# Single PSUM banks for score pairs, one exponential of 512 columns for each row half, and a rearranged table of steps

## The chip, the cores and the metric

The kernel runs on one core of a Trainium2 chip. The metric is the device time of one execution in microseconds (us). Shown are the median of timed runs and one profiled execution, whose trace the rows below are read from.

## What is computed

Four attention blocks one after the other on eight images of 32x32 tokens with 128 channels, all in float32. The first two blocks have 8 heads of 16 channels behind a group norm, the last two have one head over all 128 channels, behind a layer norm and a group norm:

```python
x = _L0_conv_ref(...)   # group norm, 8 heads: softmax(q k / 4) v, projection, + x
x = _L1_conv_ref(...)   # group norm, 8 heads, biases, + the normed x
x = _L2_conv_ref(...)   # layer norm, 1 head of 128 channels, + x
x = _L3_conv_ref(...)   # group norm, 1 head of 128 channels, + x

scores = jnp.einsum('bcq,bck->bqk', q, k) * hd ** (-0.5)
scores = jax.nn.softmax(scores, axis=-1)
o = jnp.einsum('bqk,bck->bqc', scores, v)
```

## The kernel before

A class `Plan` writes down one order of work for the whole kernel, and every engine's program walks that same list, taking from it what is its own; semaphores tie them together. The table `STEPS` is that order, one letter a step: T a score tile, P a pair, V the values of a slot, U half of them (half the columns), and C the next of everything else that the plan lists. `arranged` deals the items out by these letters.

The blocks with heads are 16 stages (an image in a block) of 4 rounds. A round is 4 heads of one half of the queries; it has 32 tiles and 8 slots. A **tile** (L1376) is one matmul on one half of the array's rows, giving scores of 128 queries by 512 keys; VectorE takes its row maxima (L1168). When a round's tiles are done, the negated maxima are turned (`shift`), split in two by ScalarE and VectorE, and written by SyncE's queue into rows of `q_stack` (four transfers, L853), where the next matmuls add them to the scores. A slot is one block of 128 keys: two **pairs**, each two matmuls (L1404), one on either half of the rows, for two heads by 512 queries. ScalarE takes the exponential of a pair, 1024 columns in one instruction (L1057), and the **values** (L1430) multiply the four probability blocks of a slot into `outs`, on four column strips side by side. The order of a pair's halves is chosen (`rows_first`) so that halves alternate along TensorE's stream and two neighbouring matmuls run side by side.

The blocks with one head are image-wide stages: **scores** (L1448, six matmuls of two halves), a maximum over 1024 columns (L1200), an exponential with its sum (L1064), eight transposes as a **turn** (L1292), a copy by ScalarE (L1073), the **pv** steps (L1470) and an output `y` by VectorE. They lie between the stages with heads, and the last 200 us hold nothing else. **Chunks** (L1292 to L1355) are the norms and projections of all blocks; their results are taken by ScalarE or VectorE.

The kernel uses eight PSUM banks of 512 columns. Three are `work`, handed out in turn to tiles, shifts, small chunks and some projections (`in_work`). Four are `pairs`, two buffers of two banks, handed out in turn to pairs, scores, turns and the other chunks (`in_pairs`); a projection of 512 columns takes a whole buffer and uses its first bank. One is `outs`. `count` gives each item its buffer and remembers who had it before; `wait_for_bank` and `wait_for_pairs` make TensorE wait until that one's reader has finished. So pair t waits for one exponential, that of the pair before it in its buffer.

## Time and profile before

| | us |
|---|---|
| median of 3 runs | 2158.66 |
| lowest, highest | 2158.46, 2170.19 |
| the profiled execution | 2159.86 |
| its span, first to last instruction | 2158.1 |

The profile gives, for this one execution, the busy time of every engine (PE is TensorE, PEld its weight loads, DVE VectorE, ACT ScalarE, POOL GpSimd, SP SyncE), who ended each wait, and the chain of work that ended last. TensorE's matmuls overlap and their ends are modelled: what a step costs is read from the start of one to the start of the next. A gap of a weight load is not time lost by itself, since loads run beside matmuls. The table of stretches has the granted clock of TensorE in its last columns but two, as a share of full speed.

### The profile page before, as it was taken

To read this page: it belongs to the slowest core of one execution; us is meant where nothing else is said; L and a number is where in the kernel's file an instruction comes from. 1 tells how busy PE (TensorE), PEld (TensorE's weight loads), DVE (VectorE), ACT (ScalarE), POOL (GpSimd) and SP (SyncE) were. 2 spreads that over 40 slices of the span, in tenths; PEclk is the share of its full clock that TensorE was granted. 3 is DMA by queue.
4 is the path that set the end of the run, shared out by engine and by line. 5 is a ranking of instruction groups with operands and counts; after the bars stand their busy time and mean duration, and the time that the engine had idled before them with its cause. 6 is when DMAs were issued, how large, how long until landed. Compare 5 with 4: busy or idle time off the path is not lost.

```text
span 2158.1 us, 39609 instructions
## 1 busy us (share of the span) xinstructions
PE 2096.4 (97%) x15750; PEld 1168.3 (54%) x15750; DVE 1687.8 (78%) x3104; ACT 1447.0 (67%) x1698; POOL 408.0 (19%) x541
## 2 busy tenths in 40 slices
PE   4999999999999999999999999999999989999999
PEld 2444444444744467444764448644584336746888
DVE  6899999999799867887679886898778957763433
ACT  1477777777577755887458874688647865586554
POOL 3102111220122311122120221213111040130221
PEclk7799999999999999999999999999999999999999
DMA  5322241331222314041230503204040050000000
GB/s 144 70 31 66 48 96 46 65 72 29 55 55 56 45 31 79 12 85 16 55 65 2 99 2 70 50 2 99 1 103 7 2 99 1 11 2 1 11 1 20
DMA packets 48583, 97.34 MB, mean 45 GB/s; under 512 B 7824, under 2 KB 10640, under 8 KB 48272
## 3 DMA queue, kind: packets, MB, share of 16 engines
q1 hardware_dynamic: 48400, 94.81, 21.0%
q8 instruction: 126, 2.06, 0.4%
q14 instruction: 57, 0.47, 0.1%
HBM read 55.98 MB, written 37.75 MB: 43 GB/s over the span
## 4 chain that ended last, share of the span: by engine, by line
PE 84%; DVE 8%; DMA 2%; issue 2%; ACT 2%; POOL 1%; SPq 1%; POOLq 0%; DVEq 0%; ACTq 0%
PE outs L1430 21%; PE work L1376 17%; PE pairs L1404 12%; PE outs L1470 11%; PE pairs L1448 8%; DVE part_max L1168 6%; PE pairs L1292 6%; PE pairs L1298 3%; PE pairs L1301 2%; PE work L1298 2%; DMA q_stack<-shift_parts 2%; PE work L1301 2%; ACT probs L1057 1%; DVE neg_max L1200 1%; SPq L853 1%
## 5 line engine op out<-in xcount | busy, mean ns | idle before, releaser
L1168 DVE TENSOR_REDUCE part_max<-work 128x1 f32<-128x512 f32 x2048 | 1282.7, 681 | 176.1 <-PE work L1376 169.6
L1057 ACT ACTIVATE probs<-pairs 128x1024 f32<-128x1024 f32 x1024 | 1002.1, 1023 | 261.2 <-PE pairs L1404 244.4
L1376 PE MATMUL work<-k_stack,q_stack 62*128 62x512 f32 x2048 | 609.7, 453 | 5.9 <-DVE part_max L1168 3.8
L1430 PE MATMUL outs<-probs,v_heads 128*32 128x512 f32 (+1 forms) x5216 | 565.8, 512 | 0.8 <-DVE o_turn L1180 0.2
L1404 PE MATMUL pairs<-q_stack,k_stack 64*128 64x512 f32 x2048 | 509.0, 446 | 15.4 <-DMA q_stack<-shift_parts 14.0
L1376 PEld LDWEIGHTS work<-k_stack,q_stack 62*128 62x128 f32 x2048 | 286.9, 187 | 316.3 <-DVE part_max L1168 233.0
L1404 PEld LDWEIGHTS pairs<-q_stack,k_stack 64*128 64x128 f32 x2048 | 224.9, 185 | 220.1 <-ACT probs L1057 128.8
L1200 DVE TENSOR_REDUCE neg_max<-pairs 128x1 f32<-128x1024 f32 x128 | 156.7, 1224 | 207.4 <-PE pairs L1448 206.7
L1064 ACT ACTIVATE probs<-pairs,neg_max 128x1024 f32<-128x1024 f32 x128 | 142.8, 1116 | 241.0 <-DVE neg_max L1200 241.0
L1470 PEld LDWEIGHTS outs<-v_full,probs 128*128 128x128 f32 x2048 | 250.8, 191 | 37.3 <-issue 28.8
L1470 PE MATMUL outs<-v_full,probs 128*128 128x128 f32 x2048 | 269.7, 279 | 0.2
L1430 PEld LDWEIGHTS outs<-probs,v_heads 128*32 128x32 f32 x5216 | 114.1, 108 | 195.2 <-issue 174.0
L1448 PE MATMUL pairs<-k_full,q_full 128*128 128x512 f32 x768 | 211.6, 411 | 4.3 <-ACT probs L1064 1.9
L945 POOL TENSOR_TENSOR o_both<-o_turn,o_inv 128x256 f32<-128x256 f32 x64 | 39.8, 621 | 752.8 <-DVE o_inv L1183 752.8
L1073 ACT COPY probs<-pairs 128x1024 f32<-128x1024 f32 x128 | 129.8, 1014 | 49.9 <-PE pairs L1292 49.8
L1448 PEld LDWEIGHTS pairs<-k_full,q_full 128*128 128x128 f32 x768 | 134.7, 188 | 49.5 <-issue 12.9
L1292 PE MATMUL pairs<-avg,probs 128*128 128x128 f32 x1024 | 133.5, 273 | 0.1
L1292 PEld LDWEIGHTS pairs<-avg,probs 128*128 128x128 f32 x1024 | 116.3, 141 | 17.6 <-issue 16.5
L967 POOL CAST parts<-parts 128x512 fp32r<-128x512 f32 x64 | 39.3, 614 | 265.9 <-ACT parts L1028 265.9
L903 POOL TENSOR_TENSOR rstd<-var_eps,minus_half 128x1 f32<-128x1 f32 (+1 forms) x32 | 26.7, 835 | 298.2 <-DVE var_eps L1131 242.6
L969 POOL TENSOR_TENSOR parts<-parts 128x512 fp32r<-128x512 f32 x64 | 82.0, 1280 | 5.1
L1180 DVE STREAM_TRANSPOSE o_turn<-outs 128x512 f32<-128x512 f32 x64 | 45.3, 708 | 9.5 <-PE outs L1430 9.5
(128 smaller groups left out, 1157.2 us busy)
## 6 DMA issues: line engine op xcount, KB each, us to landing
k_scratch<-parts SPq DMA_DIRECT2D x64, 256.0 KB
q_scratch<-parts SPq DMA_DIRECT2D x64, 256.0 KB
k_stack<-k_scratch SPq DMA_DIRECT2D x64, 256.0 KB, 6.9
q_stack<-q_scratch SPq DMA_DIRECT2D x64, 256.0 KB, 9.6
k_stack<-k_scratch SPq DMA_DIRECT2D x64, 128.0 KB, 8.1
q_stack<-q_scratch SPq DMA_DIRECT2D x64, 128.0 KB, 10.2
q_stack<-shift_parts SPq DMA_DIRECT2D x256, 4.0 KB
tmp<-x SPq DMA_DIRECT2D x7, 512.0 KB, 3.8
```

Of the source, the lines that this page charges most:

```text
L1057: nc.scalar.activation(probs[:, plan.prob[u], 2 * n:2 * n + 2, :], pairs[:, plan.half["pair", t], :, :], ACT.Exp, scale=HEAD_SCALE).then_i ...
L1064: nc.scalar.activation(p_full[:, n % 2, :], bank_of(("scores", n)), ACT.Exp, bias=neg_max1[:, n % SUMS:n % SUMS + 1], accum_out=sum1[:, n ...
L1073: nc.scalar.copy(pT_full[m % 2][:, :, P * (n % 2):P * (n % 2 + 1)], bank_of(("turn", n)).rearrange("p (k q) -> p k q", q=P)).then_inc(f_co ...
L1168: nc.vector.tensor_reduce(part_max[:, r % 2, column:column + 1], bank_of(("tile", r, n)), AX_X, ALU.max, negate=True).then_inc(tile_max, 1)
L1200: nc.vector.tensor_reduce(neg_max1[:, n % SUMS:n % SUMS + 1], bank_of(("scores", n)), AX_X, ALU.max, negate=True).then_inc(f_max, 1)
L1292: last = nc.tensor.transpose(bank[:, P * n:P * (n + 1)], source(j), ident)
L1298: return nc.tensor.matmul(to, weights, moving, start=True, stop=True)
L1376: nc.tensor.matmul(bank_of(("tile", r, n)), qs[rows, i, a, heads, P * t:P * (t + 1)], ks[rows, i, keys, heads, :], start=True, stop=True). ...
L1404: last = nc.tensor.matmul(pairs[:, plan.half["pair", t], half, :], ks[rows, i, key // QT, first + n, P * (key % QT):P * (key % QT + 1)], q ...
L1430: last = nc.tensor.matmul(outs[2 * HD * n:2 * HD * (n + 1), columns], v_heads[:, i, key, at:at + 2 * HD], probs[:, plan.prob[u], n, column ...
L1448: last = nc.tensor.matmul(pairs[:, plan.half["scores", n], half, :], q_full[:, k % 2, q, queries], k_full[:, k % 2, key, columns_of(half)] ...
L1470: last = nc.tensor.matmul(outs[:, P * j:P * (j + 1)], pT_full[m % 2][:, k, P * j:P * (j + 1)], v_full[:, at % 2, k, :], start=k == 0, stop ...
```

## The change

The seven banks that are not `outs` become one tensor `banks`. A class `Banks` hands them out, the longest unused first, by kind of item and by part of the order. In the stages with heads ("head"), tiles and their like take one of banks 4 to 6, and each half of a pair takes one of banks 0 to 3 by itself, as does a projection of 512 columns; wide chunks take two neighbours. In the image-wide stages ("full"), scores, turns and wide chunks take banks 0 and 1 or 2 and 3, a pair there takes such a double, one bank for each half, and projections go with the tiles.

A pair's halves each wait for their own bank and each count in `pair_full`; ScalarE takes one exponential of 512 columns for each half, in the order in which the matmuls come, and each counts in `exp_done`. What waits for these two semaphores waits for doubled counts.

The table of steps is rearranged, and scores (S), turns (R), pv steps (G) and y (Y) have letters of their own. Both tables hold the same items; the values split in two number 140 before and 128 after. The table is cut here to a few of its lines.

```diff
-WORK_BANKS = 3
+BANKS = 7
+SINGLES = {"head": {"work": (4, 5, 6), "exp": (0, 1, 2, 3)}, "full": {"work": (4, 5, 6)}}
+DOUBLES = {"head": ((0, 1), (1, 2)), "full": ((0, 1), (2, 3))}
...
+class Banks:
+
+    def __init__(self):
+        self.holders, self.last, self.count = [None] * BANKS, [-1] * BANKS, 0
+
+    def take(self, choices, holder):
+
+        chosen = min(choices, key=lambda banks: max(self.last[b] for b in banks))
+        before = []
+        for b in chosen:
+            if self.holders[b] is not None and self.holders[b] not in before:
+                before.append(self.holders[b])
+            self.holders[b], self.last[b] = holder, self.count
+        self.count += 1
+        return chosen, before
+
+    def take_for(self, plan, item, part):
+
+        if item[0] in ("scores", "turn"):
+            return [self.take(DOUBLES["full"], item)]
+        if item[0] == "pair" and part == "full":
+            (first, second), before = self.take(DOUBLES["full"], (*item, 1))
+            self.holders[first] = (*item, 0)
+            return [((first,), before), ((second,), before)]
+        if item[0] == "pair":
+            return [self.take([(b,) for b in SINGLES[part]["exp"]], (*item, k)) for k in range(2)]
+        if plan.in_pairs(item) and item[1] not in HALVES:
+            return [self.take(DOUBLES[part], item)]
+        user = "exp" if plan.in_pairs(item) and part == "head" else "work"
+        return [self.take([(b,) for b in SINGLES[part][user]], item)]
+
+
+def part_of(item, part):
+    return "full" if item[0] in ("scores", "turn", "pv") else "head" if item[0] == "values" else part
...
     STEPS = (
-        "TPTTPV TPTTPTV TPTPUTTU TPTPUTTU CTPTPTV TPTTUPTTU TTPPTTV CPPTTTUU PTTUTPTU TTPPTUTTU PPTTTV TTPPTV "
...
+        "TPTTPV TPTTPTV TPTPUTTU TPTPUTTU CTPTPTV TPPTTTUTTU TPPTTUU CTPPTTV PTTUTPTU TPPTTUTPTU TTPPTV TTPTV "
...
+        "PTTPV PTTTPV CSV CSTR CTTTR CTTSGSGTTTGR GSGGSGGR YTTGCGTTGGR GSGTTTGGCCYSGTTTGR GCGCR SGTTGCGTTGCR "
+        "YSGTTTGGCCGCR SGGGTTTGCYR SGGGTTGCCTTCCGR SGGTTTGCCR YSTTTGCSGR TTTGGGGGGR YTTGSTTGCCGGR TTPGGGGTYTR "
...
+        "GGCSGGGYSGCGSGGCR GGGGCYR CSGSGGGR CGCGCGCCGR YR GGGSCSGGGGR GYSGGSGGR GGGGR YCSGGGGR CSGGGGR YCCSGGGGR "
+        "CSGGGGR YCCCCSGGGGR CCSGGGGR YSGGGGR SGGGGR YSGGGGR SGGGGR YSGGGGR SGGGGR YSGGGGR GGGGR YGGGGGGGGY "
     )
...
-        queues = {n: deque(c for c in order if n == self.class_of(c)) for n in "TPC"}
+        queues = {n: deque(c for c in order if n == self.class_of(c)) for n in "TPCSRGY"}
...
-        return {"tile": "T", "pair": "P", "values": "V"}.get(item[0], "C")
+        return {"tile": "T", "pair": "P", "values": "V", "scores": "S", "turn": "R", "pv": "G", "y": "Y"}.get(item[0], "C")
...
-            if self.in_work(item):
-                bank = n % WORK_BANKS
-                n += 1
-                self.bank[item], self.before[item] = bank, held.get(bank)
-                held[bank] = item
-            elif self.in_pairs(item):
-                self.half[item] = ring % 2
-                ring += 1
-                self.pairs_before[item] = pairs_held.get(self.half[item])
-                pairs_held[self.half[item]] = item
+            part = part_of(item, part)
+            if self.in_work(item) or self.in_pairs(item):
+                taken = banks.take_for(self, item, part)
+                self.banks[item] = sum((chosen for chosen, _ in taken), ())
+                self.before[item] = [before for _, before in taken]
...
-        pairs = psum("pairs", [P, 2, 2, HALF])
+        banks = psum("banks", [P, BANKS, HALF])
         outs = psum("outs", [P, HALF])
-        work = psum("work", [P, WORK_BANKS, HALF])
...
-            if item in plan.bank:
-                return work[:, plan.bank[item], :]
-            both = pairs[:, plan.half[item], :, :]
-            return both[:, 0, :] if item[0] == "chunk" and item[1][-1] in "01" else both.rearrange("p a k -> p (a k)")
+            first, last = plan.banks[item][0], plan.banks[item][-1]
+            if first == last:
+                return banks[:, first, :]
+            return banks[:, first:last + 1, :].rearrange("p a k -> p (a k)")
+
+        def halves_of(t):
+
+            first = plan.rows_first["pair", t]
+            return first, 1 - first
...
-                        sp.wait_ge(pair_full, 2 * STAGE_SLOTS * (g - 1))
+                        sp.wait_ge(pair_full, 4 * STAGE_SLOTS * (g - 1))
...
-                    act.wait_ge(pair_full, t + 1)
-                    nc.scalar.activation(probs[:, plan.prob[u], 2 * n:2 * n + 2, :],
-                                         pairs[:, plan.half["pair", t], :, :], ACT.Exp,
-                                         scale=HEAD_SCALE).then_inc(exp_done, 1)
+                    for k, half in enumerate(halves_of(t)):
+                        act.wait_ge(pair_full, 2 * t + k + 1)
+                        nc.scalar.activation(probs[:, plan.prob[u], 2 * n + half, :],
+                                             banks[:, plan.banks["pair", t][k], :], ACT.Exp,
+                                             scale=HEAD_SCALE).then_inc(exp_done, 1)
...
+                def wait_for_banks(item, k=0):
+                    for before in plan.before[item][k]:
+                        if before[0] == "tile":
+                            pe.wait_ge(tile_max, plan.tile_nth[before] + 1)
+                        elif before[0] == "pair":
+                            pe.wait_ge(exp_done, 2 * before[1] + before[2] + 1)
+                        elif before[0] == "scores":
+                            pe.wait_ge(f_exp, before[1] + 1)
+                        elif before[0] == "turn":
+                            pe.wait_ge(f_copied, before[1] + 1)
+                        elif before[0] == "shift":
+                            pe.wait_ge(*taken(*before))
+                        else:
+                            pe.wait_ge(*taken(*before[1:]))
...
-                    wait_for_pairs(("pair", t))
-
-                    start = plan.rows_first["pair", t]
-                    for half in (start, 1 - start):
+                    for k, half in enumerate(halves_of(t)):
                         rows = slice(ROWS * half, ROWS * (half + 1))
-                        last = nc.tensor.matmul(pairs[:, plan.half["pair", t], half, :],
-                                                ks[rows, i, key // QT, first + n, P * (key % QT):P * (key % QT + 1)],
-                                                qs[rows, i, a, first + n, :], start=True, stop=True)
-                    last.then_inc(pair_full, 1)
+                        wait_for_banks(("pair", t), k)
+                        nc.tensor.matmul(banks[:, plan.banks["pair", t][k], :],
+                                         ks[rows, i, key // QT, first + n, P * (key % QT):P * (key % QT + 1)],
+                                         qs[rows, i, a, first + n, :], start=True, stop=True).then_inc(pair_full, 1)
...
-                    pe.wait_ge(exp_done, 2 * (u + 1))
+                    pe.wait_ge(exp_done, 4 * (u + 1))
```

## Rows read from the trace of the kernel before

**Rows 1.** The page: the span and the busy time of each engine.

```profile
span 2158.1 us, 39609 instructions
...
PE 2096.4 (97%) x15750; PEld 1168.3 (54%) x15750; DVE 1687.8 (78%) x3104; ACT 1447.0 (67%) x1698; POOL 408.0 (19%) x541
```

**Rows 2.** The page: the chain that ended last, by engine, then by line.

```profile
PE 84%; DVE 8%; DMA 2%; issue 2%; ACT 2%; POOL 1%; SPq 1%; POOLq 0%; DVEq 0%; ACTq 0%
...
PE outs L1430 21%; PE work L1376 17%; PE pairs L1404 12%; PE outs L1470 11%; PE pairs L1448 8%; DVE part_max L1168 6%; PE pairs L1292 6%; PE pairs L1298 3%; PE pairs L1301 2%; PE work L1298 2%; DMA q_stack<-shift_parts 2%; PE work L1301 2%; ACT probs L1057 1%; DVE neg_max L1200 1%; SPq L853 1%
```

**Rows 3.** Busy time by stretch: stretch, length, us busy of each engine, clock, DMA.

```profile
75.00:500.00 425.00, 419.23 (x3381) 182.96 (x3380) 399.92 (x719) 313.31 (x346) 74.48 (x107) 1.00 0.33 66
...
1400.00:1500.00 100.00, 99.89 (x778) 42.74 (x771) 91.66 (x163) 85.40 (x94) 19.34 (x34) 1.00 0.26 54
```

**Rows 4.** The same for the exponentials of L1057 alone.

```profile
1400.00:1500.00 100.00, 78.93 (x82) 1.00 0.26 54
```

**Rows 5.** Groups by line and shape: count, busy us, mean ns, idle before.

```profile
L1057 ACT ACTIVATE probs<-pairs 128x1024 f32<-128x1024 f32 x1024 | 1002.1, 1023 | 261.2 <-PE pairs L1404 244.4 <-PE outs L1470 11.1 <-PE outs L1430 1.5
...
L1022 ACT COPY v_full<-pairs 128x512 f32<-128x512 f32 x13 | 7.6, 587 | 2.6 <-PE pairs L1301 1.5 <-PE pairs L1298 0.8
...
L1168 DVE TENSOR_REDUCE part_max<-work 128x1 f32<-128x512 f32 x2048 | 1282.7, 681 | 176.1 <-PE work L1376 169.6
```

**Rows 6.** Who waited for whom: us in total, times, longest.

```profile
PEld work L1376 <- DVE part_max L1168: 233.0, 443, 1.2
...
PEld pairs L1404 <- ACT probs L1057: 128.8, 244, 0.9
...
PE pairs L1404 <- DMA q_stack<-shift_parts: 14.0, 6, 8.6
```

**Rows 7.** Timeline near 382 us: start, us, instruction, idle before and releaser.

```profile
380.37 3.77 ACT L1057 ACTIVATE probs<-pairs 128x1024 f32<-128x1024 f32 x4
...
382.36 0.50 PE L1404 MATMUL pairs<-q_stack,k_stack 64*128 64x512 f32 x2 [0.33 <-ACT probs L1057]
```

**Rows 8.** Timeline of TensorE and its weight loads near 408 us.

```profile
401.97 0.64 PE L1430 MATMUL outs<-probs,v_heads 128*32 128x256 f32 x8
...
402.54 0.55 PE L1376 MATMUL work<-k_stack,q_stack 62*128 62x512 f32 x2
...
404.32 0.50 PE L1376 MATMUL work<-k_stack,q_stack 62*128 62x512 f32 x2
...
404.66 0.39 PE L1404 MATMUL pairs<-q_stack,k_stack 64*128 64x512 f32 x2
...
405.21 0.16 PEld L1430 LDWEIGHTS outs<-probs,v_heads 128*32 128x32 f32 x8 [0.36 <-issue]
...
406.21 0.50 PE L1404 MATMUL pairs<-q_stack,k_stack 64*128 64x512 f32 x2
...
406.54 0.39 PE L1376 MATMUL work<-k_stack,q_stack 62*128 62x512 f32 x2
...
412.92 1.07 PE L1430 MATMUL outs<-probs,v_heads 128*32 128x512 f32 x8
...
413.91 0.73 PE L1376 MATMUL work<-k_stack,q_stack 62*128 62x512 f32 x3
```

**Rows 9.** Timeline of TensorE in two image-wide stages.

```profile
1316.71 1.04 PE L1292 MATMUL pairs<-avg,probs 128*128 128x128 f32 x8
...
1317.51 1.63 PE L1448 MATMUL pairs<-k_full,q_full 128*128 128x512 f32 x6
...
2130.95 1.04 PE L1292 MATMUL pairs<-avg,probs 128*128 128x128 f32 x8
...
2131.88 1.66 PE L1448 MATMUL pairs<-k_full,q_full 128*128 128x512 f32 x6
```

**Rows 10.** A long piece of the chain, and timeline at a first pair.

```profile
1227.44 10.40 DMA q_stack<-shift_parts
...
1774.95 0.79 PE L1404 MATMUL pairs<-q_stack,k_stack 64*128 64x512 f32 x2 [8.60 <-DMA q_stack<-shift_parts]
```

148 lines of the change are left out of this document (58 added, 90 removed).

## Prediction

> **What bounds the kernel now.** I read the page first. TensorE is busy 97% of the span, VectorE 78%, ScalarE 67% [rows 1], so TensorE is the bound and every microsecond in which it waits counts in full. Busy TensorE is not TensorE without waits, though: matmuls overlap, and a short wait disappears inside the modelled busy time. The chain that ended last shows what the waits are made of: 84% TensorE, 8% VectorE, 2% DMA, 2% ScalarE; by line the maxima of score tiles (L1168) hold 6% and the exponentials (L1057) 1% [rows 2]. The reader should see that the engine whose instructions are split here, ScalarE, has 1% of the path (some 22 us, between 11 and 32 with the rounding), and that the larger part of the waiting is for VectorE, whose work the change leaves as it is.
>
> The table by stretch says where. From 75 to 500 us VectorE is busy 399.92 of 425 us and TensorE 419.23: two engines nearly full. From 1400 to 1500 it is ScalarE that is fullest, 85.40 of 100 us [rows 3], with 82 exponentials [rows 4].
>
> **ScalarE: one exponential of 1024 columns becomes two of 512.** One of 1024 takes 1023 ns, and a 512-column copy out of the same banks 587 ns [rows 5]. Four exponentials in a row took 3.77 us [rows 7]: taking off one full length for the last, (3.77 - 1.02) / 3 = 0.92 us each, so a follower overlaps by about 0.10. A 512-column exponential should then take 0.59 alone and 0.49 in a row. A pair costs 2 x 0.49 - 0.92 = 0.06 us more where ScalarE is saturated, and at worst, with no overlap, 2 x 0.587 - 1.023 = 0.15. Over 1024 pairs that is 61 to 154 us of ScalarE time, of which I take 61, because the row of four is the case that matters. ScalarE goes from 1447 to about 1510 us, 70% of the span. In the fullest stretch it goes from 85.4 to 85.4 + 82 x 0.06 = 90.3 us of 100. What hides this is ScalarE's own idle time; the cover is gone where the extra reaches (100 - 85.4) / 82 = 0.18 us per pair, beyond the worst case above. So I put nothing on the path for it directly, only through the queue in the next term.
>
> **TensorE: two waits and two increments a pair instead of one.** A score tile already has a wait and an increment for each matmul. Two tiles that open a run took 404.66 - 404.32 = 0.34 us until the next, and the two matmuls of a pair 406.54 - 406.21 = 0.33 [rows 8]. Where both matmuls of a slot wait and count, the slot is no more than 0.01 us longer, so the second wait and increment cost 0 to 10 us over 1024 pairs; I take 0. The Trainium skill speaks against this edit: "TensorE: Matmul & The Clock Gate", section "The cost: per-tile semaphore tail", has increments of matmuls that run side by side serialise at about 26 ns each. An estimate from that page is 1024 x 0.026 = 27 us more; the rows here show at most 0.01 a pair.
>
> **The ring of single banks.** Before, a pair waits until the whole exponential of the pair two before it has ended. At 382.36 a pair waits for L1057 while four exponentials run back to back [rows 7]. After, four banks go round, and the first half's bank comes free about 0.46 us sooner than the second's; the second comes 0.06 later than now. TensorE runs its stream in order, so the wait itself still ends at the second half. What is won is that one of two matmuls is done inside it: at most about half of a 0.33 us step, less the 0.06. With 244 such waits [rows 6], 0.12 - 0.06 gives 15 us if each of them were a real one. They are not: a weight load also stands idle 0.36 us with nothing late [rows 8], and 128.8 - 244 x 0.36 = 41 us is a ceiling that the chain's 22 us lies under. The queue in front of ScalarE grows with its load, against the gain. I take -6 us; the ends are -22 (the whole share of L1057) and +22 (that share doubled). A second gain is structural: a 512-column chunk took one of two double buffers, so that by the old table 114 of 1024 pairs follow the pair directly before them in their buffer and 115 follow a chunk. In the new table, handed out by the new rule, 1573 of 2048 halves follow the fourth half before and 249 the third. Few of those places can cost anything now, since the old order kept them apart; the gain can come only through the order, which is the next term.
>
> **The table.** Tiles keep their pace: counted at every 16th slot of values, both tables have issued the same number of tiles to within 4. So nothing is shifted between stages. Three things change. Values split in two fall from 140 to 128: a half until the next run takes 402.54 - 401.97 = 0.57 us, a whole 413.91 - 412.92 = 0.99 [rows 8], so a split costs 0.15 and twelve give -2 us (0 to -4, if a run of row matmuls is cut besides). Unbroken runs of three tiles fall from 184 to 163; runs of two or more pairs rise from 161 to 185. Three tile banks and 681 ns a maximum make a run of three the place where TensorE waits for L1168. That wait is at most 233.0 - 443 x 0.36 = 74 us [rows 6, 8]; 21 of 184 runs fewer is 11% of it, -8 us. Its ends are 0 and -25, because VectorE has only 25 us of idle time in the first 425 us, where the waits are densest [rows 3]. Third, in the image-wide stages scores, turns, values and outputs now have letters of their own. Before, 105 of 128 score steps take the banks of the score step directly before them and so wait for a maximum and an exponential; after, 60 do, and 50 take a turn's. In the last stretch a turn is followed by scores after 2131.88 - 2130.95 = 0.93 us, where nothing is late after 1317.51 - 1316.71 = 0.80 [rows 9]: 0.13 us a step. 45 steps fewer would be -6; in the middle stages tiles fill part of the wait already, so I take -4 (0 to -11).
>
> **What gets later.** Round 42's shift rows are requested T13 P8 V4 ahead of their first pair where they were T17 P10 V5 ahead: by the steps above, about 0.9 us of row matmuls and 0.99 of values less. Its transfer was 10.40 us on the chain [rows 10] and hardly waited for, so this is +1 to +2, I take +1. Round 59's wait of 8.60 us [rows 10] keeps its distance of P4 V2 in both tables and stays; all such waits together are 14.0 us [rows 6]. The only other edit on SyncE is a count doubled for the doubled increments, at no cost: it is met by the same instruction.
>
> **The sum.** -6 - 2 - 8 - 4 + 1 = -19 us. The profiled execution took 2159.86 us, its span 2158.1; the median of the three runs is 2158.66, 1.2 under it. 2159.86 - 19 - 1.2 gives about 2140. As every term but one is a share of a wait that I could only bound from above, I forecast 2142.
>
> **The rivals.** *A larger gain.* The freer ring lets the new order remove half of what is left of both waits: half of 22 us of exponentials and half of 74 of maxima, 48 us, with the rest as above 2107 to 2125; say 2115. For it speaks that TensorE is the bound, so nothing else takes over; against it that VectorE has 25 us to give in the densest stretch. *Nothing measurable.* The waits that count are VectorE's, with the same three banks and the same 2048 maxima, and ScalarE's share of the path is 1%: the split values and the last stage remain, 2152. *Slower: ScalarE's queue.* Place: the dense head stretches like 1400 to 1500. There ScalarE goes to 90 of 100 us, in the worst case to 85.4 + 82 x 0.15 = 97.7; with runs of pairs up from 161 to 185 each run meets a fuller queue. If the path's share of L1057 doubles and the order brings nothing, 2158.66 + 22 = 2181. It decides from about 0.12 us extra a pair on (95 of 100 us), twice the price that I take. *Slower: the second increment.* If each pair's two increments cost the path what a slot can hide at most, 0.01 us by the rows, it is +10 on the forecast, 2152. An estimate from the Trainium skill's "TensorE: Matmul & The Clock Gate", same section, would make it 2142 + 27 = 2169.
>
> **Chances.** The forecast, a gain of 6 to 21 us, 0.40. The larger gain 0.30. Nothing measurable 0.14. ScalarE's queue 0.12, half of it past 1%. The second increment 0.04. About 1% is what a measurement of this kernel can tell from no change: 21.6 us. Faster by over 1% is all of the larger gain and a small part of the forecast's own spread, 0.34; slower by over 1% is half of ScalarE's queue and a little for what I do not see, 0.10; the rest, 0.56, within 1%. The range has to reach into the larger gain and a little past no change: 2112 to 2168. The forecast's own range is 2137 to 2153.
>
> **What the profile would show.** Right on ScalarE: 2048 exponentials of 128x512 with a mean near 590 ns, ScalarE near 1510 us busy; past 1580, the overlap is gone and the queue rival is alive. Right on the ring: the weight loads of the pairs wait for the exponentials less than 128.8 us in all, and its share of the chain stays at or under 1%. Right on the table: tile weight loads wait for L1168 less than 233.0 us, and in the last 180 us turns are followed by scores after 0.80 rather than 0.93 us. The DMA wait of 8.60 us is still there. I would be wrong if VectorE's share of the chain grows, if the pairs' runs make TensorE wait twice where it waited once (once for each half, with no row matmul of the other half to run beside), or if a transfer of shift rows that landed in time now lands late in more than one round.

## The result: 0.6% faster, and the profile after

The changed kernel takes 2147.98 us (median of 9 runs, 2142.41 to 2153.83) against 2158.66 us (9 runs): a ratio of 0.9942, 95% interval 0.9923 to 0.9961. That lies inside the forecast's own range of 2137 to 2153 us, 6 us above the forecast. The profiled execution took 2149.76 us.

The page of the changed kernel: busy time, then the chain that ended last by engine and by line. L1412 is the score tiles' matmul, L1425 the pairs', L1450 the values', L1092 the exponentials, L1203 the maxima of tiles.

```profile
span 2148.0 us, 40503 instructions
...
PE 2090.5 (97%) x15668; PEld 1166.9 (54%) x15668; DVE 1689.0 (79%) x3104; ACT 1499.1 (70%) x2722; POOL 408.0 (19%) x541
...
PE 86%; DVE 7%; DMA 2%; issue 2%; ACT 1%; SPq 1%; POOL 0%; POOLq 0%; DVEq 0%; ACTq 0%
```

Against [rows 1, 2] ScalarE is 52 us busier, VectorE's and ScalarE's shares of the path are each a point smaller. The groups of the two instructions in dispute, and the table by stretch:

```profile
L1203 DVE TENSOR_REDUCE part_max<-banks 128x1 f32<-128x512 f32 x2048 | 1282.3, 681 | 184.1 <-PE banks L1412 178.3
L1092 ACT ACTIVATE probs<-banks 128x512 f32<-128x512 f32 x2048 | 1063.7, 604 | 198.8 <-PE banks L1425 173.9
```

```profile
75.00:500.00 425.00, 421.45 (x3424) 183.04 (x3420) 402.21 (x725) 331.82 (x639) 75.07 (x108) 1.00 0.33 66
1400.00:1500.00 100.00, 98.60 (x762) 41.66 (x750) 89.58 (x160) 87.78 (x172) 21.65 (x38) 1.00 0.29 54
```

An exponential of 512 columns has a mean of 604 ns, and the group of 2048 is busy 1063.7 us where the 1024 were 1002.1 [rows 5]: 0.06 us more a pair. The dense stretch goes from 85.40 us [rows 3] to 87.78. The waits, us in total, times, longest:

```profile
PEld banks L1412 <- DVE part_max L1203: 248.7, 464, 1.2
PEld banks L1425 <- ACT probs L1092: 139.4, 257, 1.7
PEld outs L1450 <- ACT probs L1092: 48.0, 158, 0.7
...
PE banks L1425 <- DMA q_stack<-shift_parts: 16.3, 6, 8.0
```

Each of these is larger than in [rows 6], and the kernel is faster all the same. The values' wait for exponentials (48.0) was small before:

```profile
PEld outs L1430 <- ACT probs L1057: 13.0, 43, 0.4
```

A weight load that waits while the matmul ahead of it still runs costs nothing, so the sums of this view do not add up to time. For what follows the times come from two other readings. One lays two traces side by side at the same slot of work (the first values of a stage, the same score step) and reads how far apart they are. The other takes the matmuls that start 0.02 to 0.09 us after the instruction that frees their bank, and adds up how far each gap between its start and that of the matmul before goes past 0.12 us, the run of tiles that opens the kernel left out; "bound" below means this count.

**Where the time went.** Side by side, the changed kernel is 5.6 us ahead at the first values of stage 8 (931 us), in the head stages, and 6.7 at those of stage 10. It loses 3.6 us at the first values of round 42 and 1.6 at those of round 50, whose shift rows come late, and is 2.2 us ahead at the last values of the head stages. The last image-wide stages, from score step 88 to 127, take 179.1 us in place of 187.0: that brings it to 10.1.

### The profile page after: what moved, and what is told of

It is laid out like the page before. It is cut to its first block, busy times and chain, and to the rows that moved or that the text cites. A ratio compares the mean times of both kernels' runs of the same rounds, so it can differ in the third digit from the quotient of the medians.

```text
span 2148.0 us, 40503 instructions
## 1 busy us (share of the span) xinstructions
PE 2090.5 (97%) x15668; PEld 1166.9 (54%) x15668; DVE 1689.0 (79%) x3104; ACT 1499.1 (70%) x2722; POOL 408.0 (19%) x541
## 4 chain that ended last, share of the span: by engine, by line
PE 86%; DVE 7%; DMA 2%; issue 2%; ACT 1%; SPq 1%; POOL 0%; POOLq 0%; DVEq 0%; ACTq 0%
PE outs L1450 21%; PE banks L1412 17%; PE banks L1425 12%; PE outs L1490 11%; PE banks L1468 9%; PE banks L1331 6%; PE banks L1337 6%; DVE part_max L1203 5%; PE banks L1340 4%; DMA q_stack<-shift_parts 2%; ACT probs L1092 1%; SPq L887 1%; DVE stats L1141 0%; PE banks L1398 0%; DVE o_turn L1215 0%
## 5 line engine op out<-in xcount | busy, mean ns | idle before, releaser
L1203 DVE TENSOR_REDUCE part_max<-banks 128x1 f32<-128x512 f32 x2048 | 1282.3, 681 | 184.1 <-PE banks L1412 178.3
L1092 ACT ACTIVATE probs<-banks 128x512 f32<-128x512 f32 x2048 | 1063.7, 604 | 198.8 <-PE banks L1425 173.9
L1412 PE MATMUL banks<-k_stack,q_stack 62*128 62x512 f32 x2048 | 638.8, 458 | 4.2 <-DVE part_max L1203 2.0
L1450 PE MATMUL outs<-probs,v_heads 128*32 128x512 f32 (+1 forms) x5120 | 566.0, 520 | 0.6 <-DVE o_turn L1215 0.2
L1425 PE MATMUL banks<-q_stack,k_stack 64*128 64x512 f32 x2048 | 532.9, 440 | 16.9 <-DMA q_stack<-shift_parts 16.3
L1412 PEld LDWEIGHTS banks<-k_stack,q_stack 62*128 62x128 f32 x2048 | 289.4, 187 | 335.3 <-DVE part_max L1203 248.7
L1425 PEld LDWEIGHTS banks<-q_stack,k_stack 64*128 64x128 f32 x2048 | 262.6, 186 | 200.3 <-ACT probs L1092 139.4
L1099 ACT ACTIVATE probs<-banks,neg_max 128x1024 f32<-128x1024 f32 x128 | 142.8, 1116 | 257.7 <-DVE neg_max L1235 213.2
L1235 DVE TENSOR_REDUCE neg_max<-banks 128x1 f32<-128x1024 f32 x128 | 156.7, 1224 | 164.9 <-PE banks L1468 164.3
L1450 PEld LDWEIGHTS outs<-probs,v_heads 128*32 128x32 f32 x5120 | 111.9, 108 | 197.3 <-issue 142.9
L1468 PE MATMUL banks<-k_full,q_full 128*128 128x512 f32 x768 | 209.5, 408 | 1.3 <-ACT probs L1092 0.3
L1468 PEld LDWEIGHTS banks<-k_full,q_full 128*128 128x128 f32 x768 | 134.9, 189 | 36.7 <-issue 9.9
```

The source lines that it names most:

```text
L1092: nc.scalar.activation(probs[:, plan.prob[u], 2 * n + half, :], banks[:, plan.banks["pair", t][k], :], ACT.Exp, scale=HEAD_SCALE).then_inc ...
L1099: nc.scalar.activation(p_full[:, n % 2, :], bank_of(("scores", n)), ACT.Exp, bias=neg_max1[:, n % SUMS:n % SUMS + 1], accum_out=sum1[:, n ...
L1203: nc.vector.tensor_reduce(part_max[:, r % 2, column:column + 1], bank_of(("tile", r, n)), AX_X, ALU.max, negate=True).then_inc(tile_max, 1)
L1235: nc.vector.tensor_reduce(neg_max1[:, n % SUMS:n % SUMS + 1], bank_of(("scores", n)), AX_X, ALU.max, negate=True).then_inc(f_max, 1)
L1412: nc.tensor.matmul(bank_of(("tile", r, n)), qs[rows, i, a, heads, P * t:P * (t + 1)], ks[rows, i, keys, heads, :], start=True, stop=True). ...
L1425: nc.tensor.matmul(banks[:, plan.banks["pair", t][k], :], ks[rows, i, key // QT, first + n, P * (key % QT):P * (key % QT + 1)], qs[rows, i ...
```

## Experiments

The kernel before was run beside each group of kernels; its medians there were 2159.79, 2161.27, 2160.5 and 2159.6 us.

| kernel | us, median (range) | ratio to before, 95% interval |
| --- | --- | --- |
| changed | 2147.98 (2142.41 to 2153.83) | 0.9942 (0.9923 to 0.9961) |
| 1 banks and split, old table | 2166.65 (2163.91 to 2173.75) | 1.0036 (1.0023 to 1.0049) |
| 2 table alone | 2163.36 (2156.37 to 2168.14) | 1.0011 (0.9997 to 1.0024) |
| 3 before, new order at the end | 2152.94 (2146.82 to 2162.97) | 0.9972 (0.9958 to 0.9985) |
| 4 changed, old order at the end | 2149.94 (2147.19 to 2161.56) | 0.9956 (0.9943 to 0.9969) |
| 5 split on doubles | 2171.95 (2168.81 to 2175.54) | 1.0054 (1.0035 to 1.0073) |
| 6 exponentials in quarters | 2174.96 (2173.65 to 2176.35) | 1.0066 (1.0049 to 1.0083) |
| 7 four banks for tiles | 2384.68 (2382.78 to 2386.05) | 1.1035 (1.1014 to 1.1056) |
| 8 shift rows by ScalarE's queue | 2163.45 (2159.56 to 2167.94) | 1.0010 (0.9996 to 1.0025) |
| 9 reads behind the shift rows | 2129.42 (2128.62 to 2130.81) | 0.9848 (0.9827 to 0.9870) |
| 10 unsplit on single banks | 2158.59 (2153.25 to 2165.06) | 0.9986 (0.9972 to 0.9999) |
| 11 before, with the reads of 9 | 2144.82 (2143.53 to 2148.92) | 0.9927 (0.9907 to 0.9947) |
| 12 split on doubles, one wait | 2160.00 (2154.26 to 2163.78) | 0.9998 (0.9982 to 1.0014) |

**1 and 2: the two halves of the change.** Run 1 is the changed kernel with the old table and its letters, run 2 the kernel before with the new ones. The diff is that of run 1, without the table itself; run 2 has the reverse.

```diff
-        queues = {n: deque(c for c in order if n == self.class_of(c)) for n in "TPCSRGY"}
+        queues = {n: deque(c for c in order if n == self.class_of(c)) for n in "TPC"}
...
-        return {"tile": "T", "pair": "P", "values": "V", "scores": "S", "turn": "R", "pv": "G", "y": "Y"}.get(item[0], "C")
+        return {"tile": "T", "pair": "P", "values": "V"}.get(item[0], "C")
```

> The new banks and the two exponentials of 512 columns, with the table of steps of before. Theory: the banks by themselves bring little, because the old order already keeps pairs away from the places where two double buffers run short: 2153 to 2160 us, with the pairs' weight loads waiting 110 to 135 us for the exponentials (128.8 before, 139.4 after) and ScalarE near 1500 us busy. Rival, ScalarE's queue: the dearer exponentials cost the path by themselves, 2163 to 2180 us, and the values' weight loads wait 40 us or more for the exponentials (13.0 before, 48.0 after). Rival, the banks are the whole gain: 2146 to 2150 us.

> The new table of steps and its letters, on the two double buffers and the exponentials of 1024 columns of before. Theory: the order of the image-wide stages gives its gain on any banks (some 8 us in the last of them), but the new order sets pairs where the double buffers run short, and the heads lose what the last stage wins: 2152 to 2165 us, pairs' weight loads waiting for exponentials 150 us or more (128.8 before). Rival, the table is the whole gain and needs no new banks: 2146 to 2151 us. Rival, the table can't do without the banks: over 2170 us.

Neither half is worth anything alone: 7 us slower, and 4 us slower with an interval that holds no change; together 11 us faster. The change is not a sum of its parts.

Side by side, one part does add up: the last image-wide stages take 187.0 us before and in run 1, 179.1 in run 2 and in the changed kernel, so the new order there is worth 7.9 us on any banks. What does not add up is the head stages. At their last values, in one execution of each, run 1 is 10.5 us behind the kernel before, run 2 is 7.3 behind, and the changed kernel is 2.2 ahead. TensorE's waits for shift rows are not the reason: they are longest in the changed kernel (16.3 us, against 14.0 before, 14.8 in run 1 and 10.8 in run 2).

Run 1 lies in the range of the rival of ScalarE's queue, and its sign came too: the values' weight loads wait 46.8 us. But the changed kernel has 48.0 of them and is 18.7 us faster, and counted as bound waits the values come to under 2 us in run 1. So the sign does not show the rival, and no run rules out that ScalarE has a share in the 7 us. The bound waits of TensorE show a part of what happens (count, us in all):

| kernel | pair halves, for exponentials | tiles, for maxima |
| --- | --- | --- |
| before | 105, 15.3 | 137, 27.2 |
| 2 table alone | 137, 30.4 | 114, 22.8 |
| 1 banks alone | 71, 11.1 | 147, 30.8 |
| changed | 80, 12.4 | 130, 25.1 |

On doubles the new table's longer runs of pairs double the waits for exponentials; on single banks it hardly matters how the pairs lie. And the old table loses on single banks in another place. A transposing chunk there takes two neighbouring banks and waits for the later of two pair halves. The waits of that chunk in run 1, then in the changed kernel:

```profile
PEld banks L1332 <- ACT probs L1093: 10.2, 13, 1.5
...
PE banks L1332 <- ACT probs L1093: 4.8, 7, 1.1
```

```profile
PEld banks L1331 <- ACT probs L1092: 5.2, 11, 0.9
```

In run 1 TensorE itself stands still for 4.8 us, in the changed kernel for 0.4. Side by side, run 1 falls behind the kernel before in stages 8, 12, 14 and 15 (1.9, 2.8, 1.6, 2.1 us), and one such wait of a weight load, 0.7 to 1.5 us long, lies in each of them. That is not the whole of it: the kernel before has waits of 0.3 to 0.8 us at the same places, in stage 14 one as long as in run 1, and run 1 also waits longer for shift rows, by 1.1 us in stage 8, 0.9 in stage 12 and 0.4 in stage 14. The rest of its 7 us I cannot place.

**3 and 4: the order at the end.** Run 3 is the kernel before with the new table's order for all that is left after the last values; run 4 is the changed kernel with the old order there. Both deal out both tables and take the second for what the first has not yet issued:

```diff
+    SEGMENTS = [('own', ('values', 511, 0, 2)), ('other', None)]
```

> The kernel before, with its own order up to the last values (slot 511) and from there on the new table's order of what is left; banks and exponentials as before. Theory: the last image-wide stages, from the first to the last scores step after the heads 187.0 us before and 179.1 after in the traces, gain their 8 us from the order alone: 2149 to 2153 us, with scores S88 to S127 in 178.5 to 180 us. Rival, it needs the new banks too, since the projections there go with the tiles' banks: 2155 to 2159 us.

> The changed kernel with its order up to the last values (slot 511) and from there on the old table's order of what is left. Theory: it gives back 7 to 8 us, 2154 to 2157 us, so that banks, exponentials and the order of everything before the last stages are worth 2 to 4 us together. Rival, the last stages gain by the banks: under 2151 us.

The new order at the end is worth 6.9 us on the old banks (2159.79 - 2152.94). Putting the old one back costs 2.0 us where 7 to 8 were expected, and that time lies in the rival's range. The traces decide against the rival: run 3 takes 179.1 us for the last stages and run 4 takes 187.0, so the order is worth 7.9 us there on either banks. Run 4 had made up for it in the head stages, at whose last values it is 9.9 us ahead of the kernel before and the changed kernel 2.2; they have the same order, but run 4 waited 4.5 us less for shift rows (11.8 against 16.3), and what such a wait costs besides is told at run 9. The timeline shows the step that the prediction counted, 0.79 us from a turn to scores instead of 0.93 [rows 9]:

```profile
2024.82 1.04 PE L1331 MATMUL banks<-avg,probs 128*128 128x128 f32 x8
2025.61 1.63 PE L1468 MATMUL banks<-k_full,q_full 128*128 128x512 f32 x6
```

and one that it did not count. TensorE in the kernel before, while a norm is worked out:

```profile
2053.64 0.28 PE L1298 MATMUL work<-mv,avg 128*128 128x1 f32 x2
2055.07 0.35 PE L1298 MATMUL work<-var_in,avg 128*128 128x1 f32 x2 [1.15 <-POOL var_in L915]
2055.28 1.63 PE L1448 MATMUL pairs<-k_full,q_full 128*128 128x512 f32 x6
```

and the same two steps of the norm in the changed kernel, with a turn and values between them:

```profile
2042.36 0.28 PE L1337 MATMUL banks<-mv,avg 128*128 128x1 f32 x2
2042.50 1.07 PE L1331 MATMUL banks<-avg,probs 128*128 128x128 f32 x8
2043.41 1.95 PE L1490 MATMUL outs<-v_full,probs 128*128 128x128 f32 x16
2045.20 0.28 PE L1337 MATMUL banks<-var_in,avg 128*128 128x1 f32 x2
```

With scores, turns, values and outputs as letters of their own, the table can put work into the 1.4 us that the norm takes. The old letter took them all from one queue in the planner's order.

**5, 12 and 10: splitting, and single banks.** All three have the new table. Run 5 gives each pair of the head stages one double of two banks again, with split exponentials:

```diff
-        if item[0] == "pair" and part == "full":
+        if item[0] == "pair":
             (first, second), before = self.take(DOUBLES["full"], (*item, 1))
...
-        if item[0] == "pair":
-            return [self.take([(b,) for b in SINGLES[part]["exp"]], (*item, k)) for k in range(2)]
```

> The changed kernel with one edit: in the head stages a pair takes a double of two banks again, (0,1) or (2,3), and waits for both before its first matmul; the two exponentials, the two increments and the new table stay. Theory A, the single banks are what the new table needs (a half can start while the other half's bank is still held, and a chunk of 512 columns takes one bank and not two): it falls back to about the run of the table alone, 2160 to 2168 us, 10 us or more above the changed kernel, and most of the difference lies before 941 us, where table alone and changed kernel differ by 12.9 us. Theory B, what helps is the split exponential (ScalarE starts half a pair earlier and a half is done sooner): it stays within 3 us of the changed kernel, 2146 to 2151 us. Between the two, 2153 to 2158 us, each has a share.

It came out slower than the table alone and than either theory, and its trace had a flaw of its own: 1862 wait instructions more than needed. Run 12 takes them out:

```diff
                 def wait_for_banks(item, k=0):
+                    if k and plan.before[item][k] is plan.before[item][0]:
+                        return
                     for before in plan.before[item][k]:
+                        if before[0] == "pair" and before[2] == 0 and (*before[:2], 1) in plan.before[item][k]:
+                            continue
```

> The run with split exponentials on doubles again, with its waits put together: there a pair waited for both halves of the pair before, ahead of each of its matmuls, four waits in all (1913 instructions more than the changed kernel), and at 102 pairs the first matmul started 0.12 to 0.15 us after the exponential's end where it is 0.03 to 0.06 in the other kernels. Here one wait, for the later of the two exponentials, stands ahead of the first matmul. Theory A, the doubles themselves cost (release of a whole pair, a chunk of 512 columns taking two banks): the time stays above 2160 us. Theory B, a good part of the 22 us between that run and the changed kernel was the price of the extra waits: it falls to 2150 to 2160 us, and the single banks are worth what is left.

So the waits alone cost 12 us (2171.95 - 2160.00, 6 ns for each on average), and run 5 must not be read as the price of doubles. Splitting alone on doubles is 2163.36 to 2160.00, -3 us with ranges that overlap. Run 10 has single banks and no split where it can be avoided:

```diff
+                    if plan.whole[t]:
+                        act.wait_ge(pair_full, 2 * (t + 1))
+                        nc.scalar.activation(probs[:, plan.prob[u], 2 * n:2 * n + 2, :],
+                                             banks[:, low:high + 1, :], ACT.Exp,
+                                             scale=HEAD_SCALE).then_inc(exp_done, 1)
+                        return
                     for k, half in enumerate(halves_of(t)):
```

> The changed kernel with the exponentials unsplit where they can be: a pair still takes two single banks, one by one, and each half waits for its own bank only, but where the two banks lie side by side (777 of 1024 pairs) one exponential of 1024 columns reads both and gives both back at once; 247 pairs keep two of 512. Theory A, the gain of the single banks is the earlier release of the first half: with it gone for three pairs in four, the kernel loses most of the 22 us by which it beats split exponentials on doubles, and stands at 2156 to 2168 us. Theory B, the gain is that a 512-column chunk takes one bank of four and no double, and the split is only a price (0.25 us for each us of ScalarE by the run with quarters): ScalarE falls from 1499 to about 1460 us and the kernel is 7 to 12 us faster, 2136 to 2141.

Its ScalarE is 43 us less busy than in the changed kernel, and it is 10.6 us slower. By the bound waits of pair halves: table alone 30.4 us, split on doubles 31.7 (158 of them), single banks mostly unsplit 25.0 (123), both 12.4. The reading that fits is that a half that waits for its own bank gains only if that bank's exponential ends earlier, and an exponential that ends earlier only if the bank is handed on by itself. With the new table each of the two is worth 3 to 5 us alone, with ranges that overlap, and together 15.4 (2163.36 - 2147.98). The waits for shift rows speak against this order of the four (10.8, 8.2, 14.5 and 16.3 us) and so do not make it.

**6: ScalarE's price.** Each 512-column exponential is cut into two of 256, and only the second counts:

```diff
-                        nc.scalar.activation(probs[:, plan.prob[u], 2 * n + half, :],
-                                             banks[:, plan.banks["pair", t][k], :], ACT.Exp,
-                                             scale=HEAD_SCALE).then_inc(exp_done, 1)
+                        for c in (slice(0, HALF // 2), slice(HALF // 2, HALF)):
+                            last = nc.scalar.activation(probs[:, plan.prob[u], 2 * n + half, c],
+                                                        banks[:, plan.banks["pair", t][k], c], ACT.Exp,
+                                                        scale=HEAD_SCALE)
+                        last.then_inc(exp_done, 1)
```

> The changed kernel with each 512-column exponential cut once more, into two of 256 columns; only the second one counts, so banks, waits and order are those of the changed kernel and only ScalarE's time goes up. From 1023 ns for 1024 columns and 604 for 512, 256 columns should take 0.39 us, so 0.15 more a half, less what overlaps: ScalarE goes from 1499 to between 1650 and 1800 us. Theory A, ScalarE still has cover: the time rises by at most 5 us, to 2153. Theory B, ScalarE's queue is already on the path in the densest stretches, as the run of the banks alone suggests (52 us more of ScalarE, about 8 us slower, so 0.15 us per us): 150 to 300 us more of ScalarE give 22 to 45 us, 2170 to 2193, and the share of the exponentials in the chain goes past 3%.

ScalarE went to 1606.7 us only, 107.6 more, since followers overlap more than I worked out; the time rose by 27 us, 0.25 us for each us of ScalarE. The chain by engine, and the group:

```profile
PE 80%; ACT 12%; DVE 5%; issue 2%; DMA 1%; POOL 0%; SPq 0%; POOLq 0%; ACTq 0%; DVEq 0%
```

```profile
L1093 ACT ACTIVATE probs<-banks 128x256 f32<-128x256 f32 x4096 | 1178.9, 432 | 135.2 <-PE banks L1427 115.3 <-PE outs L1492 11.6 <-PE outs L1452 0.5
```

ScalarE's share of the path goes from 1% to 12%, and the bound waits of pair halves from 12.4 to 46.7 us. ScalarE's queue was a real danger, 0.105 us a pair (107.6 / 1024) past where the change stopped.

**7: one bank from the pairs to the tiles.**

```diff
-SINGLES = {"head": {"work": (4, 5, 6), "exp": (0, 1, 2, 3)}, "full": {"work": (4, 5, 6)}}
+SINGLES = {"head": {"work": (3, 4, 5, 6), "exp": (0, 1, 2)}, "full": {"work": (4, 5, 6)}}
```

> The changed kernel with one bank moved in the head stages from the pairs to the score tiles: tiles go round over four banks, pair halves over three; the table and the image-wide stages stay. Theory A, a run of three tiles waits because there are three banks (the ground on which the table was to give 8 us): the weight loads of tiles wait for the maxima less than 200 us in place of 248.7, and the kernel is 5 to 20 us faster, 2128 to 2143. Theory B, VectorE's pace and not the depth of its ring sets those waits, and the pairs need their fourth bank: the waits of the tiles fall, those of the pairs for exponentials rise from 139.4 past 200 us, and the kernel is 10 to 40 us slower, 2158 to 2190.

```profile
PEld banks L1425 <- ACT probs L1092: 415.5, 549, 1.2
...
PEld banks L1412 <- DVE part_max L1203: 199.0, 329, 1.0
```

The tiles' waits fall by 50 us, their bound waits from 25.1 to 4.1; the pairs' bound waits rise from 12.4 to 268, and the kernel is 237 us slower, where theory B had said 10 to 40. With three banks a half waits for the exponential of the pair directly before it (397 of the 420 bound waits). Three single banks are too few; with four, two pairs are in flight and 12.4 us of bound waits are left.

**8, 9 and 11: the shift rows.** Run 8 sends the shift rows of ten rounds from ScalarE's queue, two pairs later:

```diff
                         shift(item[1])
+                        if item[1] in OTHER_QUEUE:
+                            due[item[1]] = 2
                     elif kind == "pair":
                         exp(item[1])
+                        for r in list(due):
+                            due[r] -= 1
+                            if due[r] == 0:
+                                send_shift(r, act)
+                                del due[r]
```

> The changed kernel with the shift rows of ten rounds (6, 14, 15, 16, 18, 26, 34, 42, 50, 59: those that follow a large read, load or write closely) sent from ScalarE's queue, two pairs after ScalarE has copied them, in place of SyncE's, where they stand behind that read. Theory A, the waits of first pairs for shift rows (16.3 us in the changed kernel, 8.3 of them in round 59, 3.1 in round 42) lie on the path and come from the place in SyncE's queue: they fall under 4 us and the kernel is 8 to 14 us faster, 2134 to 2140. Theory B, the transfer is late because the DMA engines are busy with the read, whichever queue asks: the waits stay within 4 us of 16.3 and the time within 3 us of 2148.

The kernel is 15 us slower than the changed one, which neither theory had. The waits of rounds 34, 42 and 50 went. But round 59 still waited, and so did round 14 (2.1 us) and round 6, whose rows had gone ahead of the next stage's reads in SyncE's order and were now asked for two pairs later. TensorE's timeline at the first pairs of rounds 6 and 59:

```profile
226.51 0.80 PE L1434 MATMUL banks<-q_stack,k_stack 64*128 64x512 f32 x2 [12.78 <-DMA q_stack<-shift_parts]
...
1785.25 0.80 PE L1434 MATMUL banks<-q_stack,k_stack 64*128 64x512 f32 x2 [6.24 <-DMA q_stack<-shift_parts]
```

ScalarE may pay for sending, too: its next exponential came after 2.43 us of standing idle. For most of that it had no work, since the next pair's matmul started at 213.00 us and took 0.50; some 0.7 us are left for the sending. Its timeline and its queue's (ACTq) at round 6:

```profile
210.90 1.22 ACTq L842 DMA_DIRECT2D q_stack<-shift_parts  x1
...
212.16 1.94 ACTq L842 DMA_DIRECT2D q_stack<-shift_parts  x3
214.21 2.06 ACT L1093 ACTIVATE probs<-banks 128x512 f32<-128x512 f32 x4 [2.43 <-PE banks L1434]
```

So another queue is not enough: the transfers in flight are still there. The busy share of the DMA engines from 190 to 235 us of this run, in tenths, 40 slices:

```profile
DMA  0000034564556966977899989999999999999654
```

They are 70 to 90% busy when round 6's rows are asked for at 211 us, and at 90% or more in every slice from 217 to 231. The Trainium skill says in "DMA: Bandwidth & Descriptors", section "Issuing engines are not separate DMA queues": transfers from any engine end on the same DMA engines and interleave there. The trace agrees, with 12.78 us from another queue. Run 9 therefore changes the order alone, on SyncE:

```diff
+READ_AFTER = {7: 26, 9: 34, 11: 42, 13: 50, 15: 59}
...
-                        read(*item[1:])
+                        if item[1] in READ_AFTER and item[2] in ("k1", "q1"):
+                            later.setdefault(READ_AFTER[item[1]], []).append(item[1:])
+                        else:
+                            read(*item[1:])
                     elif kind == "shift":
                         shift(item[1])
+                        for piece in later.pop(item[1], []):
+                            read(*piece)
```

> The changed kernel with one edit in SyncE's order: the reads of the pieces k1 and q1 of stages 7, 9, 11, 13 and 15 are issued behind the shift rows of rounds 26, 34, 42, 50 and 59, which they stood ahead of; all else stays. Theory A, a first pair waits for its shift rows because the DMA engines still work off those reads (from ScalarE's queue, which had no reads ahead of it, round 59 still waited 6.5 us, while rounds 34, 42 and 50, asked for two pairs later, did not wait): the five rounds' waits (15.3 us in the changed kernel, 14.9 of them in these four: 2.3, 3.1, 1.5, 8.3) fall under 5 us, no tile waits for the reads, and the kernel is 6 to 12 us faster, 2136 to 2142. Theory B, the reads are wanted that early: tiles of the next stage wait for k1 or q1 instead, and the time stays within 3 us of 2148 or is above it.

SyncE's issues around round 59, in the changed kernel (L877 are the reads, L887 the shift rows) and then in run 9 (L878, L888):

```profile
1745.31 2.77 SPq L877 DMA_DIRECT2D k_stack<-k_scratch  x4
1748.19 1.87 SPq L877 DMA_DIRECT2D q_stack<-q_scratch  x4
1750.17 1.76 SPq L877 DMA_DIRECT2D k_stack<-k_scratch  x4
1752.03 1.78 SPq L877 DMA_DIRECT2D q_stack<-q_scratch  x4
1758.20 2.73 SPq L887 DMA_DIRECT2D q_stack<-shift_parts  x4
```

```profile
1738.47 1.78 SPq L878 DMA_DIRECT2D q_stack<-q_scratch  x4
1748.21 2.74 SPq L888 DMA_DIRECT2D q_stack<-shift_parts  x4
1751.06 1.78 SPq L878 DMA_DIRECT2D k_stack<-k_scratch  x4
1752.93 1.78 SPq L878 DMA_DIRECT2D q_stack<-q_scratch  x4
```

All five rounds' waits are gone, TensorE's wait for shift rows is 1.7 us in one place (the first round), no tile waits for the late reads, and the kernel is 18.6 us faster than the changed one, 1.5% faster than before: the fastest of the study. That is more than the waits show: side by side, rounds 34, 42, 50 and 59 gain 3.7, 4.3, 1.7 and 10.6 us, 20.3 together, where TensorE had stood idle for 2.3, 2.8, 1.3 and 8.0, or 14.3. The rest fits TensorE's clock. Behind the waits of 2.3 and 2.8 us, and from the middle of that of 8.0 us on, the changed kernel had for a stretch a granted clock of 0.50, the lower level of 1.2 GHz; behind that of 1.3 us, and in all of run 9 from 80 us on, the clock stayed at 1.00, which is 2.4 GHz. The stretches of rounds 34, 42, 50 and 59, in the columns of [rows 3]:

```profile
974.62:978.03 3.41, 3.41 (x16) 1.35 (x15) 2.38 (x5) 2.37 (x6) 0.18 (x1) 0.50 0.00 0
1234.03:1237.45 3.42, 3.42 (x15) 1.17 (x7) 2.57 (x6) 2.57 (x7) 0.62 (x1) 0.50 0.00 0
1490.50:1493.90 3.40, 3.40 (x32) 1.74 (x36) 2.64 (x6) 2.85 (x6) 0.32 (x1) 1.00 0.00 0
1766.51:1776.75 10.24, 5.44 (x24) 1.72 (x26) 2.26 (x4) 2.21 (x5) 0.62 (x1) 0.50 0.19 38
```

The same eight matmuls just before the longest wait and behind it:

```profile
1762.29 1.04 PE L1450 MATMUL outs<-probs,v_heads 128*32 128x512 f32 x8
1771.31 0.80 PE L1425 MATMUL banks<-q_stack,k_stack 64*128 64x512 f32 x2 [7.99 <-DMA q_stack<-shift_parts]
...
1772.89 1.93 PE L1450 MATMUL outs<-probs,v_heads 128*32 128x512 f32 x8
```

TensorE was busy for 12.3 us at the lower level (3.41 + 3.42 + 5.44). If half of that was lost, 6 us by this estimate, it is what the waits do not show (20.3 - 14.3). Run 11 puts the same edit on the kernel before:

> The kernel before with the edit of the reads alone: k1 and q1 of stages 7, 9, 11, 13 and 15 are issued behind the shift rows of rounds 26, 34, 42, 50 and 59. Without the waits for shift rows the two kernels show what the change itself is worth. Theory A, part of the change's gain is hidden by such waits (in the traces the changed kernel loses 3.1 us at round 42 and 1.5 at round 50 that the kernel before does not): the kernel before gains only its own waits (0.9 + 2.2 + 0.8 + 8.9 = 12.7 us), 2144 to 2149 us, and the changed kernel with the same edit, 2129.4, stays 15 to 20 us below it. Theory B, the reads cost both alike: it gains about 20 us too, to 2137 to 2142, and the change is worth 8 to 12 us as measured.

It gains 14.8 us. Without these waits the change is worth 2144.82 - 2129.42 = 15.4 us rather than 10.7; some 5 us of it were hidden.

## Why the prediction held, step by step

**The total** was right: the likeliest case, a gain of 6 to 21 us, with TensorE still the bound; 10.7 came. The terms behind it were less right than their sum, and that the sum came out so near is in part luck: too much was given to the head stages, too little to the last stages and to the late transfers.

**ScalarE's price**: right. 604 ns where 590 was said, 52 us more where 61 was said, hidden by idle time. From run 2 to run 12 ScalarE gains 58 us (1441.7 to 1499.9) and the time does not rise, though run 12 also starts its exponentials earlier, so that a small price could hide there. The rival of ScalarE's queue had its mechanism right too, as run 6 shows, and needed more load than the change brings: it was to decide from 0.12 us a pair on, and at 0.06 + 0.105 = 0.17 it costs 27 us. That is below the 0.18 us at which I had put the end of ScalarE's cover, so that end was too high.

**The second wait and increment** at 0: borne out for the increment, as far as a net result can. From run 2 to run 12 each pair gets a second increment, and the time does not rise. The rule of "TensorE: Matmul & The Clock Gate", section "The cost: per-tile semaphore tail", by which the Trainium skill speaks against them, would have given +27 us by the estimate from that page; no run here shows it. The second wait was not tested alone, since run 12 has one wait a pair. What does cost is a wait that needs an instruction of its own: 6 ns each in run 5.

**The ring at -6 us and the table at -14** (-2, -8 and -4): this is the step that failed, in its form. I priced them as terms that add. Alone they are worth +7 and +4 us (the latter within its interval), together -11. Runs 9 and 11, without late shift rows, differ by 15.4 us, and 7.7 of that lies in the last image-wide stages (186.8 against 179.1); so the ring, the splits and the tiles, priced at -16 together, were worth about half of that, and only together. The 0.12 us in my sum for the ring stands in no row either: half a step of 0.33 is 0.165. My sentence that few of the new ring's places can cost anything, since the old order kept them apart, was half of it. The other half is that the old order kept pairs apart because it had to: run 2 sets them closer and doubles their bound waits. And on the new ring a chunk of two banks must wait for two halves, which is a part of what run 1 loses.

**The tiles at -8**: wrong in its sign by the view that I named (233.0 to 248.7), and over-sized by the bound waits (27.2 to 25.1, so -2). Runs of three tiles are fewer, but the count of runs said little about how late VectorE is at each.

**The image-wide order at -4**: right in place, half the size. I counted 45 steps of 0.13 us and missed the norm's 1.4 us gaps that the new letters fill. The traces give 7.9 us with the old banks and with the new, the times of run 3 give 6.9.

**The late transfers at +1**: under-sized. TensorE waited 2.8 us at round 42 (0.6 before), with the lower clock behind it, and 1.3 at round 50, which I had not listed. Round 59 stayed, as forecast (8.0 us). Run 11 puts the loss at about 5 us.

**The signs.** ScalarE's share of the path fell as said. The pairs' weight loads were to wait less than 128.8 us and waited 139.4, while their bound waits fell from 15.3 to 12.4: the sign was taken from a view whose sums are not time. One of my signs of being wrong came true, shift rows that land late in more than one round (42 and 50); it told of that term and not of the total.

## What to carry to other kernels

Two edits that each look like a loss can be one change. If a finer buffer makes room for a different order, run all four corners, and look at what the order had been avoiding. A small transfer that work waits for belongs ahead of the large reads in the order of issue; another queue did not do that here. Such a wait can cost more than it shows, where the granted clock falls behind it. And a wait in front of a weight load is a place to look at, not a time to add up.

## What the runs showed of the hardware

The spread of the runs shrank with the same few waits: the changed kernel's 9 times lie within 11.4 us of each other, the 4 of run 9 within 2.2, the 6 of run 11 within 5.4. A DMA issue on ScalarE's queue took 0.65 to 1.2 us of that queue at a busy moment. And a 256-column exponential took 432 ns, 0.71 of one with twice the columns, yet all 4096 were busy for only 0.29 us each (1178.9 / 4096): followers overlap by a third. TensorE's granted clock went from 1.00 to 0.50 with waits of 2.3, 2.8 and 8.0 us, and stayed at 1.00 behind one of 1.3.
